# A selective-scan block with a following linear layer: where a chunk's boundary work stands on five engines

## The chip, the cores and the metric

One core of one Trainium2 chip runs the whole program. The metric is the device time of one execution in microseconds (us); a lower one is better. All data are 32-bit floats.

## The reference

For 4096 rows `x` of 1024 values, two blocks follow each other, each with a layer norm ahead of it and the block's input added behind it:

```
x = x + mamba(layernorm(x))          # in_proj -> x, z (2048 channels each)
                                     # xc = silu(causal conv, 4 taps, of x)
                                     # xc @ x_proj -> dt_r (64), B (16), C (16), each rms-normed
                                     # dt = softplus(dt_r @ dt_proj + bias)
                                     # h[t] = exp(dt*A) * h[t-1] + dt*B[t]*xc[t]   (16 states a channel)
                                     # y = (sum_n h*C + D*xc) * silu(z);  out_proj(y)
x = x + layernorm(x) @ W.T + bias    # W dequantised from codes and scales, once
```

## The kernel before

The 4096 rows are cut into 16 **chunks** of 256 rows (`T`), the 2048 channels into 8 **pairs** of 128-channel tiles. The loop runs over 16 x 8 = 128 **steps**; step `S = 8c + j` scans pair `j` of chunk `c`. `first` is j = 0, `last` is j = 7. Four chunks are in work at once: while chunk c is scanned, the step's PE work also holds the input projection and convolution of chunk c+1, the output projection of chunk c-1 and the second linear layer ("ffn") of chunk c-2. Each engine has its own stream of instructions, written out by hand in the order in which it runs; semaphores alone tie them together.

A step has 16 **units** of 512 columns. For each, ACT keeps the last state and makes two exponentials (`unit(u)`, L1107 and L1111), POOL makes the products of dt, x and B (`dbx`, L494, one for two units), DVE scans (`scan(u)`, L1416, into one of four banks `hb`) and multiplies by C (`product(u)`, L1364); `unit(u)` waits for `product(u-4)`, which frees its bank. POOL adds pairs of products (`half`, L512 and L518), and PE sums them over the identity into `ys` (`group(k)`, three for either tile, L606). The last three groups of a step stand in the next one (`late_groups`). The sum times silu(z) is the output (`y_gate`, L1375): tile 0 at the end of its own step, tile 1 early in the next (`late_y`).

PE's other work of a step, by line: `ffn` L721 (DVE adds its result, `add_ffn`, L1332), `out_proj` L799 in parts of the contraction into `g1` (`add_out`, also L1332), `x_proj` L636 (DVE: `pair_ss`, L1310 and L1313), `x_in_proj` L626 in two halves (ACT: `x_taps`, L984 to L992; DVE: `taps`, six operations on L1298), `dt_proj` L656 (ACT: `dt_softplus`, with a table load ahead and behind), and `z_in_proj` L646, the step's last, which may overwrite its bank once `y_gate(S, 0)` has read it. ACT's `silus` takes z's result early in the next step.

At a chunk's **boundary** more is done. In the last step: four transposes of a normed row block (`norm1`, L613, copied by ACT on L976), the statistics of the second norm on DVE (L1339, L1272), and the rms norm of dt, B and C (`rms_apply`, `ss_transpose`, `ss_out`), after which SP writes B and C out and loads them back over all partitions, a quarter at a time (`load_b`, `load_c`, 512 KB each). In the first step: the second norm's start (L946 to L952), its two rows into `xrow` (L959) and four transposes (`norm2`). All transposes go through bank `gx`, one after the other: each waits for ACT's copy of the one before. `edge` marks a last step with `norm1` and a first step with `norm2`. There are 13 boundaries that have both (the last steps of chunks 1 to 13).

SP issues its loads in program order and stops at each wait: what stands behind a waiting load waits as well.

Of the kernel before, what the change touches and what calls it, by code (L numbers as in the profile page):

```python
# [91 lines left out]
def build_program(nc, x, win, wout, wf_codes, wf_scales, ffn_bias, xproj, dtw_in, convw_in, convb_in,  # L92
                  alog_in, dparam_in, lnw_in, out):
    ctx = ExitStack()
    with ctx:
# [179 lines left out]
        def _(sp):  # L275
# [75 lines left out]
            def iteration(st, c):  # L351
# [4 lines left out]
                def step(j):  # L356
# [24 lines left out]
                    if first and st.norm1:  # L381
# [3 lines left out]
                        sp.dma_start(xrow[:], x_rows[c + 2]).then_inc(xrow_in, 16)  # L385
                    if last and st.inproj:
                        bc_rows(c + 1)
                        for q in range(2):
                            load_b(c + 1, q)
                            load_c(c + 1, q)  # L390
                    if nx.x_job(nx_last):
                        load_pair(S + PAIRS + 2)
# [206 lines left out]
        def _(pe):  # L599
# [95 lines left out]
            def iteration(st, c):  # L695
                def step(j):
# [86 lines left out]

                    def out_proj(part):
                        if not st.outproj:
                            return
                        if part == 0:
# [7 lines left out]
                        for kt in range(part * TILES // 4, (part + 1) * TILES // 4):  # L795
# [8 lines left out]
                        if part == 3:  # L804
                            mm.then_inc(o_mm, 1)
# [16 lines left out]
                    if last and st.norm1:  # L822
                        norm1(0)
                        x_proj()
                        out_proj(0)
                        norm1(1)
                        out_proj(1)
                        norm1(2)
                        out_proj(2)
                        norm1(3)  # L830
                        x_in_proj(0)
                        ss_transpose()
                        out_proj(3)
                        dt_proj()
                        x_in_proj(1)
                        group(0)
                        group(1)
                        group(2)
                    elif first and st.ffn:
                        out_proj(0)  # L840
                        out_proj(1)
                        x_proj()
                        out_proj(2)
                        norm2(0)
                        out_proj(3)
                        norm2(1)
                        group(0)
                        dt_proj()
                        norm2(2)
                        group(1)  # L850
                        norm2(3)
                        x_in_proj(0)
                        group(2)
                        x_in_proj(1)
                    else:
                        out_proj(0)
                        out_proj(1)
# [7 lines left out]
                        out_proj(2)  # L865
                        group(2)
                        out_proj(3)
                    z_in_proj(1)
# [70 lines left out]
        def _(act):  # L939
# [144 lines left out]
            def iteration(st, c):  # L1084
                def step(j):
# [88 lines left out]
                    def norm2_row(tt):  # L1174
                        if first and st.ffn:

                            act.wait_ge(l1_tr, after(4 * min(c + 2, NC)))
                            norm2_rows(c - 2, tt)

# [21 lines left out]
                    unit(0)  # L1201
                    unit(1)
                    unit(2)
                    norm2_start()
                    unit(3)
# [4 lines left out]
                    first_skip_term()  # L1210
                    norm1(0)
                    unit(5)
                    norm1(1)
                    rms_square()
                    unit(6)
                    norm2_row(0)
                    norm1(2)
                    unit(7)
                    norm2_row(1)
                    norm1(3)  # L1220
                    unit(8)
                    norm2(0)
                    rms_apply()
                    norm1_start()
                    unit(9)
                    norm2(1)
                    norm1_row(0)
                    unit(10)
                    ss_out()
                    norm2(2)  # L1230
                    norm1_row(1)
                    unit(11)
                    norm2(3)
                    unit(12)
                    if not edge:
                        x_taps()
# [4 lines left out]
                    unit(14)  # L1241
                    if edge:
                        x_taps()
                    unit(15)

                steps(c, step)
# [3 lines left out]
            LAST = NC * PAIRS  # L1250
            norm2_begin(NC - 2)
            act.wait_ge(l1_tr, after(4 * NC))
            act.wait_ge(l2_tr, after(4 * (NC - 2)))
            for tt in range(TT):
                norm2_rows(NC - 2, tt)
            act.wait_ge(f_mm, after(LAST - 2 * PAIRS))
# [11 lines left out]
        def _(dve):  # L1268
# [128 lines left out]
            def iteration(st, c):  # L1397
                def step(j):
# [112 lines left out]
                    product(11)  # L1511
                    y_gate(S, 0)
                    if not edge:
                        taps()
# [6 lines left out]
                    if edge:  # L1521
                        taps()
                    scan(15)
# [84 lines left out]
```

## Time and profile before

| | |
|---|---|
| median of 3 runs | 4553.35 us (4550.11 to 4554.59) |
| profiled execution: time / span | 4553.78 us / 4552.0 us |
| a plain step (2, 3, 4, 6) of chunks 2 to 13, median | 32.26 us |
| last step, median | 37.16 us |
| first step, median | 35.98 us |
| second step, median | 33.58 us |
| PE busy / DVE busy, share of the span | 94% / 91% |
| first scan / last scan's end | 130.3 us / 4411.7 us |

A step's length is the distance between the starts of its first scan and of the next step's. The times in the rows are microseconds from the span's start. A row by stretch has the stretch and its length, the busy us (and count) of PE, PE's weight loads, DVE, ACT and POOL, the mean granted clock, the DMA engines' busy share and GB/s. A row of a timeline has start, duration, engine, line and instruction, count, and the idle time before it with what ended it; PE's counts are passes, two for each matmul, and neighbours overlap by 0.1 to 0.2 us. PE = TensorE matmul, DVE = VectorE, ACT = ScalarE, POOL = GpSimd, SP = SyncE.

### The profile page before, as it was taken

What the parts mean: (1) busy time and instruction counts of PE and PEld (TensorE: products, weight loads), DVE (VectorE), ACT (ScalarE), POOL (GpSimd) and SP (SyncE); (2) the same over time, 40 slices, a digit from 0 to 9 for tenths busy, and PEclk for the clock granted to TensorE, in tenths of its full rate; (3) what the DMA queues carried; (4) which work ended last, traced back from release to release, by engine and by line L of the source; (5) the groups of instructions that cost most, each with busy time, mean ns of one, the idle gap of its engine ahead of it and who ended that gap; (6) DMA issues with size and microseconds to landing.
All of it is one profiled execution on the core that took longest, in us unless ns stands there. A gap on an engine that the chain in (4) does not pass through costs nothing.

```text
span 4552.0 us, 77871 instructions
## 1 busy us (share of the span) xinstructions
PE 4257.0 (94%) x25632; PEld 3830.9 (84%) x25632; DVE 4156.6 (91%) x5745; ACT 3534.8 (78%) x8848; POOL 3887.0 (85%) x2894
## 2 busy tenths in 40 slices
PE   7688989999999999999999999999999999998879
PEld 6567778888888888888888888988888898897769
DVE  3899999999999999999999999999999999999871
ACT  3788787888888788787888888787888878888750
POOL 0898989989898998989899898998989899899870
PEclk9788999999999999999999999999999999998889
DMA  7545556575756657575575757557575665755452
GB/s 247 160 122 184 150 183 184 164 224 174 220 166 196 192 174 220 163 227 163 176 218 165 234 155 219 175 156 242 155 226 168 209 189 147 226 167 178 133 150 85
DMA packets 201348, 828.91 MB, mean 182 GB/s; under 512 B 25456, under 2 KB 34416, under 8 KB 151792
## 3 DMA queue, kind: packets, MB, share of 16 engines
q1 hardware_dynamic: 141296, 639.35, 38.6%
q0 software_dynamic: 41216, 151.01, 18.7%
q10 hardware_dynamic: 18432, 33.56, 2.0%
q8 instruction: 204, 3.34, 0.3%
q14 instruction: 200, 1.64, 0.1%
HBM read 634.57 MB, written 55.05 MB: 151 GB/s over the span
## 4 chain that ended last, share of the span: by engine, by line
PE 60%; POOL 19%; DVE 10%; issue 7%; ACT 2%; DMA 1%; SPq 0%; POOLq 0%; DVEq 0%; ACTq 0%
PE ys L646 14%; POOL dbx L494 12%; PE gx L626 12%; PE ys L606 12%; PE g L799 10%; PE g L721 7%; DVE hb L1416 6%; POOL half L518 3%; POOL half L512 3%; DVE gx L1298 1%; PE ys L636 1%; PE hb L901 1%; DVE hc L1364 1%; DMA ybuf<-in_wf_scales 1%; POOL hd L507 1%
## 5 line engine op out<-in xcount | busy, mean ns | idle before, releaser
L494 POOL TENSOR_TENSOR dbx<-dtx,bb 128x1024 f32<-128x1024 f32 x1024 | 2427.4, 2370 | 231.1 <-DVE hb L1416 183.8
L1416 DVE TENSOR_TENSOR_SCAN hb<-hb,dbx 128x512 f32<-128x512 f32 x2048 | 2495.6, 1219 | 55.4 <-ACT hb L1111 27.3
L1111 ACT ACTIVATE hb<-dt,a_neg 128x256 f32<-128x256 f32 x4096 | 1789.1, 468 | 66.3
L606 PE MATMUL ys<-half,ident 128*128 128x256 f32 x3072 | 811.6, 400 | 162.6 <-POOL half L512 93.6
L799 PEld LDWEIGHTS g<-wo,ybuf 128*128 128x128 f32 x7680 | 919.2, 194 | 30.7 <-issue 14.7
L646 PE MATMUL ys<-xnT,wz 128*128 128x256 f32 x4096 | 926.2, 385 | 11.4 <-DVE ybuf L1375 11.4
L799 PE MATMUL g<-wo,ybuf 128*128 128x128 f32 x7680 | 928.3, 277 | 8.4 <-issue 8.4
L626 PE MATMUL gx<-xnT,wx 128*128 128x256 f32 x3968 | 895.4, 383 | 21.5 <-issue 10.9
L646 PEld LDWEIGHTS ys<-xnT,wz 128*128 128x128 f32 x4096 | 782.6, 193 | 127.8 <-DVE ybuf L1375 22.8
L626 PEld LDWEIGHTS gx<-xnT,wx 128*128 128x128 f32 x3968 | 750.6, 192 | 127.3 <-issue 14.3
L606 PEld LDWEIGHTS ys<-half,ident 128*128 128x128 f32 x3072 | 567.4, 195 | 302.2 <-POOL half L512 125.0
L1107 ACT COPY hstate<-hb 128x2 f32<-128x2 f32 x2044 | 319.0, 156 | 646.1 <-DVE hc L1364 549.3
L518 POOL TENSOR_TENSOR half<-hc 128x512 f32<-128x512 f32 x512 | 651.3, 1272 | 97.0 <-DVE hc L1364 96.8
L1364 DVE TENSOR_TENSOR hd<-hb,cb 128x512 f32<-128x512 f32 x1024 | 688.4, 672 | 0.0
L1364 DVE TENSOR_TENSOR hc<-hb,cb 128x512 f32<-128x512 f32 x1024 | 688.0, 672 | 0.0
L721 PEld LDWEIGHTS g<-wf,x2nT 128*128 128x128 f32 x3552 | 414.1, 192 | 5.7
L721 PE MATMUL g<-wf,x2nT 128*128 128x128 f32 x3552 | 414.5, 275 | 0.0
L512 POOL TENSOR_TENSOR half<-hd 128x512 f32<-128x512 f32 x256 | 326.0, 1273 | 2.5 <-DMA hd<-hd 2.4
L1298 DVE SCALAR_TENSOR_TENSOR gx<-xpre,convw,gx 128x256 f32<-128x256 f32 x744 | 302.2, 481 | 23.2 <-ACT gx L992 23.2
L507 POOL DMA_DIRECT2D hd<-hd x256 | 227.9, 890 | 21.4 <-DVE hd L1364 7.6
L537 POOL TENSOR_TENSOR dtx<-dt,xcs 128x510 f32<-128x510 f32 x128 | 202.4, 1581 | 0.0
L1375 DVE TENSOR_TENSOR ybuf<-ys,gate 128x256 f32<-128x256 f32 x256 | 107.4, 419 | 99.7 <-PE ys L606 95.0
(108 smaller groups left out, 3145.5 us busy)
## 6 DMA issues: line engine op xcount, KB each, us to landing
wz<-in_win SPq DMA_DIRECT2D x128, 1024.0 KB, 5.0
hd<-hd POOLq DMA_DIRECT2D x256, 512.0 KB, 6.3
wx<-in_win SPq DMA_DIRECT2D x124, 1024.0 KB, 5.0
wo<-in_wout SPq DMA_DIRECT2D x123, 1024.0 KB, 7.3
wf<-wf_scratch SPq DMA_DIRECT2D x113, 512.0 KB, 3.6
xc_scratch<-xcn ACTq DMA_DIRECT2D x128, 256.0 KB, 2.7
xcs<-xc_scratch SPq DMA_DIRECT2D x128, 256.0 KB, 5.2
bb<-bc_scratch SPq DMA_DIRECT2D x64, 512.0 KB, 9.6
```

What stands on the lines that cost most here:

```text
L494: nc.gpsimd.tensor_tensor(dbx[:, k % 2, :].rearrange("p (n t) -> p n t", n=NQ), dtx[:, S % 2, a, :].unsqueeze(1).to_broadcast([P, NQ, T]), ...
L512: nc.gpsimd.tensor_tensor(sum_place(SUMS * S + PAIR_SUM[a]), hd[:, 2 * a, 0:HALF], hd[:, 2 * a, HALF:GW], ALU.add).then_inc(halves, 1)
L518: nc.gpsimd.tensor_tensor(sum_place(SUMS * S + LATER_SUMS[a][i]), hc[:, i, 0:HALF], hc[:, i, HALF:GW], ALU.add).then_inc(halves, 1)
L606: mm = nc.tensor.matmul(ys[i // 3][:, 0:T], ident[:], half[:, n % PLACES, w * T:(w + 1) * T], start=False, stop=(i % 3 == 2 and w == 1), s ...
L626: mm = nc.tensor.matmul(pair_bank(q)[:, a * T:(a + 1) * T], pair_weights(q)[:, kk, a * P:(a + 1) * P], xnT[:, chunk % 2, kk, :], start=(kk ...
L646: mm = nc.tensor.matmul(ys[0][:, a * T:(a + 1) * T], wz[:, kk, a * P:(a + 1) * P], xnT[:, q // PAIRS % 2, kk, :], start=(kk == 0), stop=(k ...
L721: mm = nc.tensor.matmul(g1[:, tt * P:(tt + 1) * P], x2nT[:, kk, tt * P:(tt + 1) * P], wf[:, kk, :], start=(kk == 0), stop=(kk == KH - 1))
L799: mm = nc.tensor.matmul(g1[:, tt * P:(tt + 1) * P], ybuf[:, (1 - st.parity) * PAIRS + kt // 2, (kt % 2) * T + tt * P:(kt % 2) * T + (tt + ...
L1111: ins = nc.scalar.activation(h[:, m * T:(m + 1) * T], dt[:, j % 2, a, :], ACT.Exp, scale=a_neg[:, ds((2 * j + a) * N + 2 * v + m, 1)])
L1298: nc.vector.scalar_tensor_tensor(bank[:, a * T:(a + 1) * T], xpre[:, a, tap:tap + T], convw[:, ds((2 * jq + a) * KC + tap, 1)], bank[:, a ...
L1364: nc.vector.tensor_tensor(dst[:, w * UW:(w + 1) * UW], hb[u % 4][:], cb[:, n:n + 2, :].rearrange("p n t -> p (n t)"), ALU.mult).then_inc(h ...
L1416: nc.vector.tensor_tensor_scan(h[:], h[:], dbx[:, k % 2, w * UW:(w + 1) * UW], 0.0, ALU.mult, ALU.add).then_inc(scans, 1)
```

## The change

Four streams are reordered; no arithmetic is added or removed.

- **PE, last step:** the third part of the output projection is split around the last transpose; the second half of the input projection follows the first directly; the fourth part goes from ahead of `dt_proj` to behind the groups, just ahead of z.
- **PE, first step:** the transposes of the second norm start the step's own part, one ahead of each part of the output projection; `x_proj` moves behind the third transpose; the fourth part goes to the end, ahead of z.
- **ACT:** the second norm's start and first row move from the first step to the end of the last one; its second row moves to behind `unit(1)`; its copies move from units 8 to 11 to units 4 to 7. In the last step `x_taps` moves from behind `unit(14)` to behind `unit(12)`.
- **DVE, edge steps:** `y_gate(S, 0)` moves from behind `product(11)` to behind `product(12)`, and `add_out` with the statistics from behind `product(12)` to behind `product(13)`. In the last step the taps move from behind `product(13)` to behind `product(11)`.
- **SP, last step:** the order is B0 B1 C0 B2 C1 B3, wo, dtw, C2, wx, C3, wz; before it was B0 C0 B1 C1, wx, wo, dtw, B2 C2 B3 C3, wz.

```diff
                     if last and st.inproj:
                         bc_rows(c + 1)
-                        for q in range(2):
-                            load_b(c + 1, q)
-                            load_c(c + 1, q)
-                    if nx.x_job(nx_last):
+                        load_b(c + 1, 0)
+                        load_b(c + 1, 1)
+                        load_c(c + 1, 0)
+                        load_b(c + 1, 2)
+                        load_c(c + 1, 1)
+                        load_b(c + 1, 3)
+                    if not last and nx.x_job(nx_last):
                         load_pair(S + PAIRS + 2)
...
                     if last and st.inproj:
-                        for q in range(2, NQ):
-                            load_b(c + 1, q)
-                            load_c(c + 1, q)
+                        load_c(c + 1, 2)
+                    if last and nx.x_job(nx_last):
+                        load_pair(S + PAIRS + 2)
+                    if last and st.inproj:
+                        load_c(c + 1, 3)
...
-                    def norm2_start():
+                    def norm2_first_row():
+                        if last and st.outproj:
+                            norm2_begin(c - 1)
+                            act.wait_ge(l1_tr, after(4 * min(c + 3, NC)))
+                            norm2_rows(c - 1, 0)
+                    def norm2_second_row():
                         if first and st.ffn:
-                            norm2_begin(c - 2)
+                            norm2_rows(c - 2, 1)
...
                     scan(12)
                     product(11)
-                    y_gate(S, 0)
                     if not edge:
+                        y_gate(S, 0)
+                    if not edge or last:
                         taps()
                     scan(13)
                     product(12)
-                    add_out()
-                    norm_stats()
+                    if edge:
+                        y_gate(S, 0)
+                    else:
+                        add_out()
+                        norm_stats()
                     scan(14)
                     product(13)
                     if edge:
+                        add_out()
+                        norm_stats()
+                    if edge and not last:
                         taps()
```

PE's rows of one last step and the following first step (`g<-wo` is the output projection, `gx<-ident,xrow` the transposes, `gx<-xnT,wx` and `ys<-xnT,wz` the two input projections, `ys<-half` the groups). Before:

```order
274 L799 MATMUL g<-wo,ybuf 128x128 x8
275 L613 MATMUL gx<-ident,xrow 128x128 x4
276 L626 MATMUL gx<-xnT,wx 128x256 x8
277 L663 MATMUL ys<-ident,ssn 97x128 x2
278 L799 MATMUL g<-wo,ybuf 128x128 x8
279 L656 MATMUL ys<-ssmT,dtw 128x256 x2
280 L626 MATMUL gx<-xnT,wx 128x256 x8
281 L606 MATMUL ys<-half,ident 128x256 x6
282 L646 MATMUL ys<-xnT,wz 128x256 x16
```

The same place in the changed kernel:

```order
275 L806 MATMUL g<-wo,ybuf 128x128 x4
276 L619 MATMUL gx<-ident,xrow 128x128 x4
277 L806 MATMUL g<-wo,ybuf 128x128 x4
278 L632 MATMUL gx<-xnT,wx 128x256 x8
279 L669 MATMUL ys<-ident,ssn 97x128 x2
280 L632 MATMUL gx<-xnT,wx 128x256 x8
281 L662 MATMUL ys<-ssmT,dtw 128x256 x2
282 L612 MATMUL ys<-half,ident 128x256 x6
283 L806 MATMUL g<-wo,ybuf 128x128 x8
284 L652 MATMUL ys<-xnT,wz 128x256 x16
```

The groups (L606, now L612) no longer stand directly ahead of z; a part of the output projection is between them. DVE's rows of the same last step, from scan 12's product on (`hb<-hb,dbx` is a scan, `ybuf` the gate, `gx<-xpre` the taps). Before:

```order
628 L1364 TENSOR_TENSOR hd<-hb,cb 128x512
629 L1375 TENSOR_TENSOR ybuf<-ys,gate 128x256
630 L1416 SCALAR_TENSOR_TENSOR hb<-hb,dbx 128x512
631 L1364 TENSOR_TENSOR hc<-hb,cb 128x512
632 L1332 TENSOR_TENSOR x<-g,x 128x2x128
633 L1339 BN_STATS bst<-x 128x6 x2
634 L1272 BN_AGGR mv<-bst 128x2 x2
635 L1416 SCALAR_TENSOR_TENSOR hb<-hb,dbx 128x512
636 L1364 TENSOR_TENSOR hc<-hb,cb 128x512
637 L1298 SCALAR_TENSOR_TENSOR gx<-xpre,convw,gx 128x256 x6
```

In the changed kernel:

```order
628 L1369 TENSOR_TENSOR hd<-hb,cb 128x512
629 L1303 SCALAR_TENSOR_TENSOR gx<-xpre,convw,gx 128x256 x6
630 L1421 SCALAR_TENSOR_TENSOR hb<-hb,dbx 128x512
631 L1369 TENSOR_TENSOR hc<-hb,cb 128x512
632 L1380 TENSOR_TENSOR ybuf<-ys,gate 128x256
633 L1421 SCALAR_TENSOR_TENSOR hb<-hb,dbx 128x512
634 L1369 TENSOR_TENSOR hc<-hb,cb 128x512
635 L1337 TENSOR_TENSOR x<-g,x 128x2x128
636 L1344 BN_STATS bst<-x 128x6 x2
637 L1277 BN_AGGR mv<-bst 128x2 x2
```

The gate now stands behind the six taps, a scan and a product. On ACT, at the end of a last step (`xrow<-x` is the second norm's row, the copies of L1107 and L1115 start a unit), the changed kernel has:

```order
883 L1119 ACTIVATE hb<-dt,a_neg 128x256 x2
884 L954 ACTIVATE nmr<-mv 128x2
885 L955 ACTIVATE rstd<-mv,eps_ln 128x2
886 L957 ACTIVATE rstd<-rstd 128x2
887 L960 ACTIVATE nmr<-nmr,rstd 128x1 x2
888 L967 ACTIVATE xrow<-x,nmr,rstd 128x1024
889 L1115 COPY hstate<-hb 128x2
890 L1119 ACTIVATE hb<-dt,a_neg 128x256 x2
```

Rows 884 to 888 stood in the first step before; now they are ahead of that step's first exponentials (row 890).

## Rows read from the trace of the kernel before

**Rows 1.** The page: the chain that ended last, by engine.
```profile
PE 60%; POOL 19%; DVE 10%; issue 7%; ACT 2%; DMA 1%; SPq 0%; POOLq 0%; DVEq 0%; ACTq 0%
```

**Rows 2.** By stretch: a plain step, chunk 7's last, chunk 8's first and second.
```profile
2342.00:2374.30 32.30, 31.89 (x199) 29.13 (x198) 32.14 (x45) 25.96 (x65) 30.15 (x23) 1.00 0.56 165
2236.00:2273.30 37.30, 35.98 (x232) 32.55 (x231) 33.77 (x51) 30.32 (x80) 30.64 (x24) 1.00 0.56 176
2273.30:2308.50 35.20, 31.59 (x191) 27.71 (x190) 31.95 (x44) 30.93 (x76) 31.73 (x26) 1.00 0.99 331
2308.50:2342.10 33.60, 33.19 (x207) 30.51 (x207) 32.21 (x46) 26.10 (x65) 30.08 (x23) 1.00 0.61 187
```

**Rows 3.** Timeline of PE, that boundary: start, us, instruction, count, idle before and releaser.
```profile
2250.88 3.69 PE L626 MATMUL gx<-xnT,wx 128*128 128x256 f32 x16 [0.72 <-issue]
2254.63 1.95 PE L799 MATMUL g<-wo,ybuf 128*128 128x128 f32 x16
2260.74 2.75 PE L606 MATMUL ys<-half,ident 128*128 128x256 f32 x12
2264.01 7.17 PE L646 MATMUL ys<-xnT,wz 128*128 128x256 f32 x32 [0.52 <-DVE ybuf L1375]
2271.02 3.73 PE L721 MATMUL g<-wf,x2nT 128*128 128x128 f32 x32
...
2302.28 7.07 PE L646 MATMUL ys<-xnT,wz 128*128 128x256 f32 x32
```

**Rows 4.** Timeline of DVE, the same boundary.
```profile
2236.13 1.22 DVE L1416 TENSOR_TENSOR_SCAN hb<-hb,dbx 128x512 f32<-128x512 f32 x1
2254.80 1.23 DVE L1416 TENSOR_TENSOR_SCAN hb<-hb,dbx 128x512 f32<-128x512 f32 x1 [1.13 <-ACT hb L1111]
2256.53 1.22 DVE L1416 TENSOR_TENSOR_SCAN hb<-hb,dbx 128x512 f32<-128x512 f32 x1
2263.53 0.42 DVE L1375 TENSOR_TENSOR ybuf<-ys,gate 128x256 f32<-128x256 f32 x1 [1.77 <-PE ys L606]
2269.23 2.43 DVE L1298 SCALAR_TENSOR_TENSOR gx<-xpre,convw,gx 128x256 f32<-128x256 f32 x6
2273.30 1.22 DVE L1416 TENSOR_TENSOR_SCAN hb<-hb,dbx 128x512 f32<-128x512 f32 x1
```

**Rows 5.** Timeline of ACT, the same boundary.
```profile
2258.12 1.28 ACT L1038 ACT_TABLE_LOAD   x1
2261.39 0.16 ACT L1107 COPY hstate<-hb 128x2 f32<-128x2 f32 x1
2264.18 0.18 ACT L984 COPY xpre<-xhist 128x6 f32<-128x6 f32 x1
2266.00 0.17 ACT L1107 COPY hstate<-hb 128x2 f32<-128x2 f32 x1
2274.42 0.19 ACT L946 ACTIVATE nmr<-mv 128x2 f32<-128x2 f32 x1
2275.57 0.16 ACT L1107 COPY hstate<-hb 128x2 f32<-128x2 f32 x1
2276.66 1.28 ACT L1117 ACT_TABLE_LOAD   x1
2283.74 1.23 ACT L959 ACTIVATE xrow<-x,nmr,rstd 128x1024 f32<-128x1024 f32 x1
```

**Rows 6.** PE in chunk 0's last step, chunk 1's last, and a stretch of that.
```profile
369.54 6.54 PE L626 MATMUL gx<-xnT,wx 128*128 128x256 f32 x16 [0.81 <-issue]
627.03 3.30 PE L606 MATMUL ys<-half,ident 128*128 128x256 f32 x8 [2.35 <-POOL half L512]
628.00:631.40 3.40, 3.40 (x12) 2.62 (x12) 1.99 (x4) 3.34 (x7) 2.50 (x2) 0.51 0.27 100
```

**Rows 7.** Waits of POOL for B: the third quarter at boundaries 7 and 9.
```profile
2278.47 0.21 POOL L472 TENSOR_TENSOR bb<-carried,inflow 128x4 f32<-128x4 f32 x1 [0.71 <-DMA bb<-bc_scratch]
2815.57 0.21 POOL L472 TENSOR_TENSOR bb<-carried,inflow 128x4 f32<-128x4 f32 x1 [2.00 <-DMA bb<-bc_scratch]
```

More of the change, by code:

```diff
@@ L782, in z_in_proj, with out_proj @@
                         pair_z(S + 1, a)
-                    def out_proj(part):
+                    def out_proj(lo, hi):
                         if not st.outproj:
                             return
-                        if part == 0:
+                        if lo == 0:
                             pe.wait_ge(wo_in, landed(PAIRS // 2 + S - PAIRS + 1))
@@ L794, in out_proj @@
                                 g1_after_o()
-                        for kt in range(part * TILES // 4, (part + 1) * TILES // 4):
+                        for kt in range(lo, hi):
                             for tt in range(TT):
@@ L803, in out_proj @@
                                                       stop=(kt == TILES - 1), skip_group_check=True)
-                        if part == 3:
+                        if hi == TILES:
                             mm.then_inc(o_mm, 1)
@@ L824, in step @@
                         x_proj()
-                        out_proj(0)
+                        out_proj(0, 4)
                         norm1(1)
-                        out_proj(1)
+                        out_proj(4, 8)
                         norm1(2)
-                        out_proj(2)
+                        out_proj(8, 10)
                         norm1(3)
+                        out_proj(10, 12)
                         x_in_proj(0)
                         ss_transpose()
-                        out_proj(3)
+                        x_in_proj(1)
                         dt_proj()
-                        x_in_proj(1)
                         group(0)
@@ L838, in step @@
                         group(2)
+                        out_proj(12, 16)
                     elif first and st.ffn:
-                        out_proj(0)
-                        out_proj(1)
+                        norm2(0)
+                        out_proj(0, 4)
+                        norm2(1)
+                        out_proj(4, 8)
+                        norm2(2)
                         x_proj()
[L843 to L846, printed above, removed]
+                        norm2(3)
+                        out_proj(8, 12)
+                        x_in_proj(0)
                         group(0)
                         dt_proj()
-                        norm2(2)
+                        x_in_proj(1)
                         group(1)
-                        norm2(3)
-                        x_in_proj(0)
                         group(2)
-                        x_in_proj(1)
+                        out_proj(12, 16)
                     else:
-                        out_proj(0)
-                        out_proj(1)
+                        out_proj(0, 4)
+                        out_proj(4, 8)
                         x_proj()
@@ L864, in step @@
                         group(1)
-                        out_proj(2)
+                        out_proj(8, 12)
                         group(2)
-                        out_proj(3)
+                        out_proj(12, 16)
                     z_in_proj(1)
@@ L1168, in norm1 @@
                             norm_evac(xnT[:, st.parity], 4 * (c + 2), i, gx, l1_tr, l1_evac)
-                    def norm2_start():
-                        if first and st.ffn:
-                            norm2_begin(c - 2)
[L1174 to L1178, printed above, removed]
+                    def norm2_first_row():
[4 more added lines that the diff above has]
+                    def norm2_second_row():
+                        if first and st.ffn:
+                            norm2_rows(c - 2, 1)
                     def norm1_start():
@@ L1202, in step @@
                     unit(1)
+                    norm2_second_row()
                     unit(2)
-                    norm2_start()
                     unit(3)
@@ L1211, in step @@
                     norm1(0)
+                    norm2(0)
                     unit(5)
                     norm1(1)
+                    norm2(1)
                     rms_square()
                     unit(6)
-                    norm2_row(0)
                     norm1(2)
+                    norm2(2)
                     unit(7)
-                    norm2_row(1)
                     norm1(3)
+                    norm2(3)
                     unit(8)
-                    norm2(0)
                     rms_apply()
@@ L1229, in step @@
                     ss_out()
-                    norm2(2)
                     norm1_row(1)
                     unit(11)
-                    norm2(3)
                     unit(12)
-                    if not edge:
+                    if not edge or last:
                         x_taps()
@@ L1241, in step @@
                     unit(14)
-                    if edge:
+                    if edge and not last:
                         x_taps()
                     unit(15)
+                    norm2_first_row()
                 steps(c, step)
@@ L1250, in _ @@
             LAST = NC * PAIRS
[L1251 to L1255, printed above, removed]
+            norm2_rows(NC - 2, 1)
             act.wait_ge(f_mm, after(LAST - 2 * PAIRS))
@@ L1511, in step @@
                     product(11)
-                    y_gate(S, 0)
                     if not edge:
+                        y_gate(S, 0)
+                    if not edge or last:
                         taps()
@@ L1521, in step @@
                     if edge:
+                        add_out()
+                        norm_stats()
+                    if edge and not last:
                         taps()
```

1 line of the change is left out of this document (removed).

## The prediction

> **What bounds the kernel now.** The page's chain comes first: 60% of the time that ended last is PE, 19% POOL, 10% DVE [rows 1]. That is an average. The stretches say more [rows 2]. In a plain step PE is busy 31.9 of 32.3 us and DVE 32.1: both are full, and nothing that only moves work can help there. In the last step PE is busy 36.0 of 37.3 and DVE 33.8; in the first, 31.6 and 32.0 of 35.2; in the second, 33.2 and 32.2 of 33.6. So over these three steps PE has about 100.8 us of work in 106.1, DVE 97.9. At most 5.3 us a boundary can be had (13 boundaries, 69 us, 1.5%), PE is the scarcer of the two, and a wait taken from DVE and given to PE is a loss.
>
> The timelines of one boundary (chunk 7 to 8) show where the 5.3 us go. On PE [rows 3]: 0.72 ahead of the first half of `x_in_proj`, which waits for ACT's copy of the last transpose, and 0.52 ahead of z, which waits for the gate; the rest lies in the first step (POOL's sums, the normed row, copies) up to z at 2302.28. On DVE [rows 4]: 1.13 at scan 9 behind ACT's `rms_apply`, 1.77 at the gate, which waits for group 2, PE's last before z.
>
> **The change, part by part.** I replay the boundary with the durations of its own rows. A unit on DVE (scan and product) is 1.72 (2254.80 to 2256.53) [rows 4].
>
> *Last step, PE up to the groups.* The last transpose stands half a part earlier. A part of `out_proj` starts at 2254.63 and lasts 1.8 net of the overlap with its successor [rows 3], so it is 0.9 earlier; its copy on ACT is then bound by the unit ahead of it and comes 0.7 earlier, and the other half part covers the wait of 0.72. `x_in_proj` starts at 2250.15 for 2250.88. Its halves (3.5 each, 3.69 with the overlap [rows 3]) and the small transpose run on to 2257.5. `dt_proj` (0.9) and the groups (2.6 net [rows 3]) end at 2261.0, for 2263.5. The part behind them ends at 2262.8.
>
> *Last step, ACT and DVE.* ACT's unit 8 and `rms_apply` come 0.7 earlier. DVE's scan 9 starts at 2254.07 for 2254.80. Four units later, at 2260.95, DVE is at the taps. ACT's `x_taps` waits for `x_in_proj`, 2257.5, and takes 1.8 (2264.18 to 2266.00 [rows 5]); the table load, softplus and load that now follow take 3.3 (2258.12 to 2261.39 [rows 5]), unit 13 another 1.1: its exponentials are there at 2263.8. DVE's taps take 2.35 (six operations, 2.43 with the overlap [rows 4]), to 2263.3; it waits 0.5, does scan 13 and product 12, and the gate ends at 2266.0. Before, it ended at 2263.95.
>
> *So z starts at 2266.05 for 2264.01, and PE waits 3.2 us ahead of it* where it waited 0.52. This is the price of the later gate: 2.35 of taps and 1.7 of unit are now ahead of a result for which PE stands still.
>
> *The clock.* PE lost its clock in chunk 1 after shorter waits: a wait of 2.35 was followed by a stretch at a granted clock of 0.51, that is 1.2 for 2.4 GHz, in which two groups and the next lines up to 631.4 were stretched; the two groups alone took 3.30 [rows 6] for 1.9 (three take 2.75 [rows 3]). I take 1.5 us for the fall, from that difference of 1.4 and a little work behind it. The bounds are nothing (no fall, and the sum is 0.25 better at each boundary, no more, since ACT is late there too) and 3.0: in chunk 0's last step, behind several waits between small matmuls, half of an `x_in_proj` took 6.54 [rows 6] for 3.69 [rows 3]. The Trainium skill, page "TensorE: Matmul & The Clock Gate", Part 1, says that half rate is the array's default and that only activity releases the gate. The rows agree, and by either a new wait of PE costs more than its length.
>
> *The second norm's first row.* DVE's statistics end at 2269.7, and its step at 2271.3 (two units and the gate's shifts). ACT waits for the statistics, then needs 1.15 for the norm's start (2274.42 to 2275.57 [rows 5]), 1.15 for a row (1.23 with the overlap [rows 5]) and 1.05 for unit 0: first scan at 2273.1. DVE waits 1.8 us there, which it never did, and the last step comes out at 37.0, as long as before (2236.13 to 2273.30 [rows 4]): what the earlier taps give, the row takes. Behind it ACT runs without a break: unit 1, second row, units 2 and 3 to 2277.15, the two table loads and the silus 3.7 (2276.66 on [rows 5]) to 2280.9, unit 4 and the skip term to 2282.3, and the copy of the first transpose to 2282.9.
>
> *First step, PE.* From 2266.05: z 7.0 (to 2271.02 from 2264.01), ffn 3.55, late groups 2.7 [rows 3], the fall 1.5: 2280.8. First transpose to 2281.25; the first part must wait for DVE's late gate, 2281.35; it ends at 2283.2, and the copy is there. Transpose, part, transpose, `x_proj` end at 2286.9. DVE stands at `pair_ss` from 2286.4: a wait of 0.5 that is new, since `x_proj` is later by half a step's front. From scan 6 at 2287.25 DVE has seven units to 2299.3, waits 0.4 for ACT's unit 13 (softplus as before), scan and product, and the gate ends at 2301.85. PE, with no normed row to wait for (1.2 before) and all copies in time, has its last part done at 2301.5. z starts at 2301.9 for 2302.28 [rows 3]: 0.4 gained, 0.1 of it lost again to restarting PE behind a wait. The second step is then PE's, as before (33.2 of 33.6 busy [rows 2]), and passes the gain on.
>
> *B's rows.* At this boundary POOL waited 0.71 for B's third quarter; at boundary 9, 2.00 [rows 7]. I counted all 13, these two being rows of them: 0.71 is the least, 1.5 the mean. The third quarter now has 1.5 MB ahead of it instead of 2 MB of rows and 2 MB of weights, is issued by 2258 and is needed at 2276: the wait goes at every boundary. My replay of boundary 7 has it covered already; the others gain the further 0.8 on average, because their first step is that much longer (median 35.98, here 35.2). What moves behind: wo has 3 MB ahead of it as before; wx and C2 are issued some 6 us later and needed 15 us after that. I cost them at nothing; if wx were late, the first half of `x_in_proj` would wait, us for us.
>
> **Sum.** 0.3 + 0.8 = 1.1 us at each of 13 boundaries: 14 us. Against it stand two edges outside them: chunk 0's last step has no output projection to fill PE, so the later gate delays z by nearly 4 us there, and in chunk 15's first step likewise; I take 1.5 us for each, less than the delay, since DVE bounds what follows. 4553.8 - 14 + 3 = 4542.8 us for the profiled execution; it stands 0.4 above the median, so 4543 (rounded up, as a replay leaves out small latencies).
>
> **Rivals.** A difference of 9 us, 0.2%, is about what measurement can tell from none.
> 1. *PE's wait decides: slower.* The fall lasts longer, or z starts later still. Another 1.5 to 1.7 us on z, ffn or groups passes on whole from 2280.8 on, since PE leads the chain there: late gate, scan 3, `x_proj`, scan 6. Per boundary 1.1 - 1.7 = -0.6; 13 x 0.6 + 3 = 11: 4564 us. The gain is gone once the fall costs 2.4 us for my 1.5. For it: chunk 0's 6.54 [rows 6]. Against: a single wait amid dense work, as here, had the short one.
> 2. *Only B's rows count.* The replay's 0.3 is nothing or -0.4; then 0.8 x 13 - 3 less up to 5: 4545 to 4551, no difference.
> 3. *No fall, and the edges cost nothing.* 1.35 x 13 = 17.5: 4536.
> 4. *PE is filled.* If DVE's order fitted PE's, the 5.3 us would go: 4553 - 13 x 4 = 4501. Against it stands the gate behind taps and unit.
> 5. *B's rows don't come earlier,* because POOL's accumulating transfers share the engines with them. Then 0.3 x 13 - 3 = 1: 4553, no change. Against it: 2.00 us of wait [rows 7] behind 4 MB of SP's own, of which 2.5 MB are now behind B. The Trainium skill, "DMA: Bandwidth & Descriptors", Issuing engines are not separate DMA queues, says that DMAs issued by all engines run on the same 16 DMA engines and interleave; no run here shows yet how far that goes.
>
> **Chances.** Forecast (4538 to 4547) 0.38; rival 1 0.24; rivals 2 and 5 0.20; rival 3 0.13; rival 4 0.05. Faster by over 0.2%: four fifths of the forecast's 0.38 (its upper end is above 4544), rivals 3 and 4: 0.50 rounded. Slower: 0.23. Same, the rest: 0.27. The range reaches from between rivals 3 and 4 to near rival 1: 4528 to 4562.
>
> **What would show it.** In the changed trace: a wait of PE ahead of z in the last step of 3 us, with a granted clock near 0.5 behind it (right), or under 1.5 (the gate is earlier than I say); last step 37.0, first 34.5, second 33.9; DVE's first scan of the first step behind ACT by 1.8; no wait of POOL for B's third quarter; scan 9's wait 1.0; DVE at `pair_ss` 0.5. I am wrong if the clock's fall lasts longer, if ACT gets the statistics much earlier than 2269.7, or if a load moved back (wx, C3) is awaited.

## The result, and the profile after

The change made the kernel slower: 4605.39 us (median of 5, 4598.50 to 4613.16) against 4553.35 (median of 5, 4550.11 to 4557.14); ratio 1.0113, interval 1.0102 to 1.0124. The forecast was 4543, and the time lies outside its range. The profiled execution took 4600.62 us (span 4598.8), 46.8 of span more than before.

The page's chain of the changed kernel, by engine, for [rows 1], and one of its groups:

```profile
PE 57%; POOL 23%; issue 8%; DVE 7%; ACT 3%; DMA 1%; SPq 0%; POOLq 0%; DVEq 0%; ACTq 0%
...
L518 POOL TENSOR_TENSOR half<-hd 128x512 f32<-128x512 f32 x256 | 325.7, 1272 | 66.2 <-DMA hd<-hd 66.2
```

POOL has grown by 4 points. Its sum of a pair (`pair_sum`, L518) now waits 66.2 us in all for the accumulating DMA hd<-hd. Before, the sum of a pair hardly waited for it (0.1 us on average at a boundary, 5.0 now). The same boundary as in [rows 2], chunk 7's last step and chunk 8's first and second:

```profile
2258.94:2295.98 37.04, 33.68 (x202) 30.15 (x202) 33.62 (x51) 31.64 (x84) 32.37 (x24) 0.95 0.57 184
2295.98:2330.91 34.93, 34.26 (x217) 31.35 (x216) 31.80 (x43) 29.69 (x72) 29.58 (x26) 1.00 0.92 316
2330.91:2369.54 38.63, 35.50 (x209) 31.82 (x208) 32.20 (x45) 26.10 (x65) 30.36 (x23) 0.96 0.59 172
```

The last two steps of the three were forecast as 34.5 and 33.9. The first step is 0.4 off; the second is 5 us longer than before, with a granted clock of 0.96. Timeline of PE there, for [rows 3]:

```profile
2288.85 8.86 PE L652 MATMUL ys<-xnT,wz 128*128 128x256 f32 x32 [3.28 <-DVE ybuf L1380]
...
2317.26 3.62 PE L632 MATMUL gx<-xnT,wx 128*128 128x256 f32 x16
...
2324.93 7.17 PE L652 MATMUL ys<-xnT,wz 128*128 128x256 f32 x32 [0.54 <-DVE ybuf L1380]
2331.95 3.73 PE L727 MATMUL g<-wf,x2nT 128*128 128x128 f32 x32
2335.52 1.03 PE L612 MATMUL ys<-half,ident 128*128 128x256 f32 x4
2339.68 3.30 PE L612 MATMUL ys<-half,ident 128*128 128x256 f32 x8 [3.13 <-POOL half L518]
```

The wait of 3.28 ahead of z is the forecast one. That of 3.13 in the second step is not: two groups of `half` stand still behind POOL and then take 3.30. Two stretches of PE behind the two waits (columns as in [rows 2]; the clock is the third number from the end):

```profile
2289.30:2292.70 3.40, 3.40 (x10) 2.69 (x9) 3.33 (x8) 0.29 (x3) 2.50 (x3) 0.51 1.04 284
2339.60:2343.00 3.40, 3.33 (x10) 2.42 (x11) 0.00 (x0) 0.39 (x1) 3.40 (x3) 0.62 0.48 184
```

Both times PE, having stood still, went on slowly: at a granted clock of 0.51 in the first of these stretches, 1.2 for 2.4 GHz, and of 0.62 on average in the second. What POOL waited for, by the timelines of POOL and of the DMAs that SP issues:

```profile
2320.47 1.21 POOL L531 DMA_DIRECT2D x<-in_ffn_bias  x1
...
2323.56 1.37 POOL L513 DMA_DIRECT2D hd<-hd  x1
...
2338.36 1.26 POOL L518 TENSOR_TENSOR half<-hd 128x512 f32<-128x512 f32 x1 [5.14 <-DMA hd<-hd]
```

```profile
2320.91 0.33 SPq L280 DMA_DIRECT2D wx<-in_win  x1
2324.42 0.33 SPq L399 DMA_DIRECT2D wo<-in_wout  x1
```

And the same place before:

```profile
2295.53 1.17 POOL L525 DMA_DIRECT2D x<-in_ffn_bias  x1
...
2298.62 1.34 POOL L507 DMA_DIRECT2D hd<-hd  x1
```

```profile
2302.48 0.33 SPq L280 DMA_DIRECT2D wx<-in_win  x1
2302.86 1.19 SPq L395 DMA_DIRECT2D wo<-in_wout  x1
```

Before, POOL had issued both of its transfers (the bias of 1024 KB, hd of 512 KB) before SP loaded wx (1024 KB), 3.9 us behind the second. Now wx goes out 0.4 us behind the bias and ahead of hd: the second half of `x_in_proj`, which frees its buffer, ends at 2320.9. From issue to landing the accumulation hd<-hd takes, before and after:

```profile
DMA to landing us min/median/max: 8.7/8.7/8.7
```

```profile
DMA to landing us min/median/max: 14.7/14.7/14.7
```

and the bias 8.0 and 13.6. hd lands at 2323.6 + 14.7 = 2338.3, where `pair_sum` starts. What the DMA engines moved in between is seen by queue: packets, MB, share of the 16 engines' time (a packet counts whole in the stretch in which it starts, so this can pass 100%). `q1` holds SP's loads, `q0 software_dynamic` POOL's transfers. Before, from 2299 to 2304, while the bias moves:

```profile
q0 software_dynamic: 276, 1.07, 107.4%
```

After, from 2321.2 to 2325.3, just behind the bias and wx, and from 2328 to 2332, when wo is under way too:

```profile
q1 hardware_dynamic: 116, 0.94, 76.3%
```

```profile
q0 software_dynamic: 104, 0.43, 53.1%
q1 hardware_dynamic: 100, 0.82, 50.6%
```

In the first of the two only SP's queue moves, and that is wx: its first packet comes 1.0 us behind its issue, the first of the bias 5.2 us behind its own (4.9 to 5.2 at the 13 boundaries, by the packets of the trace; 1.9 to 3.4 before). In the second the bias shares the engines with wo. hd, next in POOL's queue, lands 4.2 us behind the bias. The list of waits of the changed kernel (total, times, longest):

```profile
PE ys L652 <- DVE ybuf L1380: 58.4, 34, 5.1
...
POOL half L518 <- DMA hd<-hd: 66.2, 15, 5.6
```

Over the 13 boundaries, last steps are shorter by 2.9 us in sum, first steps by 13.7, second steps longer by 61.0 (4.7 each); the rest of the span is longer by 2.4. Together 46.8. The forecast passed over a column of [rows 2]: in chunk 8's first step the DMA engines were busy for 0.99 of the time, in its neighbours for 0.56 and 0.61.

### The profile page after: what moved, and what is told of

The parts are those of the page before. It is cut to its first block, busy times and chain, and to the rows that moved or that the text cites. A ratio compares the mean times of both kernels' runs of the same rounds, so it can differ in the third digit from the quotient of the medians.

```text
span 4598.8 us, 77871 instructions
## 1 busy us (share of the span) xinstructions
PE 4279.0 (93%) x25632; PEld 3859.2 (84%) x25632; DVE 4154.7 (90%) x5745; ACT 3535.2 (77%) x8848; POOL 3886.5 (85%) x2894
## 4 chain that ended last, share of the span: by engine, by line
PE 57%; POOL 23%; issue 8%; DVE 7%; ACT 3%; DMA 1%; SPq 0%; POOLq 0%; DVEq 0%; ACTq 0%
PE ys L652 15%; POOL dbx L500 14%; PE ys L612 11%; PE g L806 10%; PE gx L632 9%; PE g L727 7%; DVE hb L1421 4%; POOL half L524 4%; POOL half L518 3%; PE ys L642 1%; POOL hd L513 1%; PE hb L909 1%; DVE hc L1369 1%; DVE gx L1303 1%; DMA ybuf<-in_wf_scales 1%
## 5 line engine op out<-in xcount | busy, mean ns | idle before, releaser
L652 PE MATMUL ys<-xnT,wz 128*128 128x256 f32 x4096 | 947.5, 391 | 58.4 <-DVE ybuf L1380 58.4
L612 PE MATMUL ys<-half,ident 128*128 128x256 f32 x3072 | 816.7, 403 | 172.4 <-POOL half L518 111.4
L806 PEld LDWEIGHTS g<-wo,ybuf 128*128 128x128 f32 x7680 | 932.2, 195 | 23.7 <-issue 5.0
L652 PEld LDWEIGHTS ys<-xnT,wz 128*128 128x128 f32 x4096 | 795.5, 197 | 179.2 <-DVE ybuf L1380 68.8
L806 PE MATMUL g<-wo,ybuf 128*128 128x128 f32 x7680 | 939.6, 278 | 2.1 <-issue 0.6
L1115 ACT COPY hstate<-hb 128x2 f32<-128x2 f32 x2044 | 318.6, 156 | 683.2 <-DVE hc L1369 516.5
L612 PEld LDWEIGHTS ys<-half,ident 128*128 128x128 f32 x3072 | 576.4, 198 | 310.1 <-POOL half L518 142.0
L518 POOL TENSOR_TENSOR half<-hd 128x512 f32<-128x512 f32 x256 | 325.7, 1272 | 66.2 <-DMA hd<-hd 66.2
```

What stands on the lines that cost most here:

```text
L518: nc.gpsimd.tensor_tensor(sum_place(SUMS * S + PAIR_SUM[a]), hd[:, 2 * a, 0:HALF], hd[:, 2 * a, HALF:GW], ALU.add).then_inc(halves, 1)
L612: mm = nc.tensor.matmul(ys[i // 3][:, 0:T], ident[:], half[:, n % PLACES, w * T:(w + 1) * T], start=False, stop=(i % 3 == 2 and w == 1), s ...
L652: mm = nc.tensor.matmul(ys[0][:, a * T:(a + 1) * T], wz[:, kk, a * P:(a + 1) * P], xnT[:, q // PAIRS % 2, kk, :], start=(kk == 0), stop=(k ...
L806: mm = nc.tensor.matmul(g1[:, tt * P:(tt + 1) * P], ybuf[:, (1 - st.parity) * PAIRS + kt // 2, (kt % 2) * T + tt * P:(kt % 2) * T + (tt + ...
```

## The experiments

Two theories. **A:** the load of wx slows POOL's transfers, hd lands late, POOL and PE wait in the second step; z's wait costs little. **B:** z's wait and the clock behind it, both in the last step, are the loss. The first expectation names a third, **C:** hd lands late because POOL issues it later. Each run was timed beside the kernel before (its medians there: 4552.53 for e1 to e4, 4553.51 for e5 to e8, 4549.94 for e9 and e10).

**e1, wx issued later by one product.** In the changed kernel, ahead of `load_pair` (wx):

```diff
+                        if first and st.ffn:
+                            sp.wait_ge(hcs, after(UNITS * S + 12))
                         load_pair(S + PAIRS + 2)
```

> The changed kernel, but in each first step SP waits for DVE's product 11 before it issues the load of wx (and so wo behind it), some 4 us later than the changed kernel does. Theory A (collision): wx and wo, issued right behind POOL's bias transfer, slow that transfer and the accumulation behind it, for which pair_sum of the second step waits 5 us. Then the accumulation's flight falls from 14.7 us to 10 to 12, the second step from 38.8 to 35 to 37, and the time to 4555 to 4580. Theory B (the gate): PE's wait of 3.3 us ahead of z and the clock's fall behind it cost the 50 us; then nothing changes here, 4600. Theory C: the accumulation is late because POOL issues it 2 us later; nothing changes here either.

Measured: 4570.73 (ratio 1.0042, 1.0027 to 1.0057). wx goes out 1.4 us later on average, not 4, and wo no later; hd's flight falls from 14.5 to 13.0 (means), the second step's median from 38.8 to 36.0. That small shift turns the order round: wx now goes out 2.0 us behind the bias (0.4 before this edit), and the bias has its first packet 1.9 us behind its issue, ahead of wx's. The bias's flight falls from 14.2 to 10.7, and wx's rises from 5.8 to 11.4.

**e2, wx issued behind the gate.** The same place, another wait:

```diff
+                        if first and st.ffn:
+                            sp.wait_ge(y_ready, after(2 * S + 1))
                         load_pair(S + PAIRS + 2)
```

> The changed kernel, but in each first step SP waits for the gate of tile 0 before it issues the load of wx, some 6.5 us later than the changed kernel. Theory A: the accumulation's flight falls to about 9 us as in the kernel before, PE's wait in the second step (2.2 to 3.6 us) is gone or under 0.5, the second step is 34 to 35, and the time 4540 to 4556; a smaller part of it can come back as a wait of PE for wo. Theories B and C: 4600, as PE's wait ahead of z in the last step (3.3 us) is untouched.

Measured: 4547.19 (0.9988, 0.9979 to 0.9998). wx goes out 4.4 us later than in the changed kernel, and wo, which stands behind it, 1.2 us. POOL's wait for hd, in the list of waits, is down to a quarter, and the second step (the stretch below) to 33.93 in the median:

```profile
POOL half L520 <- DMA hd<-hd: 16.4, 15, 2.4
```

```profile
2301.23:2335.56 34.33, 33.84 (x209) 30.67 (x208) 32.20 (x46) 26.09 (x65) 30.39 (x23) 1.00 0.65 207
```

One wait in SP's queue gives 58 us back (4605.39 - 4547.19), with the later gate untouched. POOL issues the bias and hd as late in the first step as in the changed kernel (24.8 us into it on average, 24.5 there, for the bias), so C is out.

**e3, the gate of last steps back behind product 11.** In the changed kernel:

```diff
                     scan(12)
                     product(11)
-                    if not edge:
+                    if not edge or last:
                         y_gate(S, 0)
-                    if not edge or last:
                         taps()
                     scan(13)
                     product(12)
-                    if edge:
+                    if edge and not last:
                         y_gate(S, 0)
-                    else:
+                    if not edge:
                         add_out()
                         norm_stats()
```

> The changed kernel, but in the last steps the gate of tile 0 stands behind product 11 again, ahead of the taps; first steps keep the later gate. PE's wait of 3.3 us ahead of z and the clock's fall behind it should go. Theory B: 4540 to 4560. Theory A: z comes 3 us earlier, but the first step is held by ACT's row and its copies, so it gains 0.3 to 0.5 us at most, and the collision in the second step stays: 4595 to 4603.

Measured: 4595.68 (1.0097, 1.0081 to 1.0112). z's wait is gone, and little is won: PE's timeline shows it wait in the first step instead, for ACT, and go on slowly (a part of `out_proj` takes 3.33; it is 1.95 elsewhere):

```profile
2299.89 0.66 PE L619 MATMUL gx<-ident,xrow 128*128 128x128 f32 x4 [2.11 <-ACT xcn L1009]
2300.38 3.33 PE L806 MATMUL g<-wo,ybuf 128*128 128x128 f32 x16
```

B is out as the main cause.

**e4, the kernel before with only SP's new order in last steps.** Its diff is the SP part of the change.

> The kernel before, with only SP's new order in the last steps (B's rows ahead of the weights). By my prediction POOL's wait for B's third quarter (1.5 us on average) is gone, the first step falls from 35.98 to about 35.2 and the time to 4543 to 4546. Rival: the wait was covered on the whole, or another load is now late, and the time stays at 4553.

Measured: 4540.98 (0.9977, 0.9967 to 0.9986). The waits of POOL for B's rows, before and here:

```profile
POOL bb L472 <- DMA bb<-bc_scratch: 27.5, 24, 2.4
```

```profile
POOL bb L477 <- DMA bb<-bc_scratch: 4.5, 8, 2.0
```

SP's order alone is worth 4552.53 - 4540.98 = 11.6 us. The median of the first step falls by 0.8, from 35.98 to 35.21, as forecast. In the profiled execution, though, which is 13.1 us shorter, the steps of the 13 boundaries give only 7.8 of it, 0.6 a boundary (chunk 2's first step is 2.1 longer), and 4.0 lie ahead of the first scan and behind the last one, where this edit changes nothing.

**e5, e2 and e3 together.**

> Two edits to the changed kernel at once: in first steps SP waits for the gate of tile 0 before it loads wx, and in last steps that gate stands behind product 11 again, ahead of the taps. If the collision and PE's wait ahead of z were two separate costs, this gives the first's 58 us and the second's 10 us: 4537. If, as I hold, PE then only waits later, for ACT's silus in the first step (2.1 us, seen with the gate alone), the second edit is worth 0 to 5 us here: 4542 to 4548.

Measured: 4541.89 (0.9974, 0.9965 to 0.9984). That is 5.3 us less than e2, at the lower edge of what the second theory said, and the intervals of the two overlap. It cannot be told from e4: all that moved on PE, ACT and DVE is worth nothing yet.

**e6, e5 with the second norm behind ACT's units.** The norm's start and first row leave the front of the first step, where DVE waited 1.82 us for ACT:

```diff
                     unit(0)
                     unit(1)
-                    norm2_second_row()
+                    norm2_first_row()
                     unit(2)
                     unit(3)
+                    norm2_second_row()
...
                     unit(15)
-                    norm2_first_row()
```

> The kernel of the two edits, and on ACT the second norm's start and first row move from the end of the last step to behind unit 1 of the first step, the second row to behind unit 3. Theory: the first step is led by ACT's chain from the statistics over row, units 0 to 3 and silus to the first transpose; units 0 and 1 now run while ACT would wait for the statistics, so the silus come some 2 us earlier, DVE's first scan doesn't wait (1.8 us), the last step is 35.0 to 35.5, and 13 boundaries gain 1 to 2 us each: 4518 to 4534. Rival: PE or POOL's sums take over at once, and it stays within 5 us of the kernel of the two edits.

Measured: 4551.35 (0.9992, 0.9982 to 1.0002). Missed. The last step is 34.93, as expected, but hd is late again: at the boundary from chunk 3 to 4 POOL's timeline has

```profile
1214.74 1.35 POOL L515 DMA_DIRECT2D hd<-hd  x1
...
1231.29 1.26 POOL L520 TENSOR_TENSOR half<-hd 128x512 f32<-128x512 f32 x1 [6.91 <-DMA hd<-hd]
```

although wx goes out 1.3 us behind hd (at 1216.07), the same distance as in e2. So the order of hd and wx alone does not decide; over the boundaries the second step runs from 33.3 to 41.3 with the same order. SP's timeline there shows other loads just ahead of the bias (which goes out at 1211.65):

```profile
1206.96 0.38 SPq L371 DMA_DIRECT2D x<-in_x  x1
1207.44 0.41 SPq L376 DMA_DIRECT2D xcs<-xc_scratch  x1
1207.95 0.38 SPq L380 DMA_DIRECT2D wf<-wf_scratch  x1
1208.41 0.60 SPq L385 DMA_DIRECT2D xrow<-in_x  x1
```

The load of x goes out 4.7 us ahead of the bias here, 10.5 us ahead in e2 (chunk 8's first step), and in the 4 us behind the bias's issue the engines moved nothing but SP's queue:

```profile
q1 hardware_dynamic: 446, 1.57, 104.5%
```

At seven boundaries wf's load is in flight for 2 us or more behind the bias's issue; there the bias's first packet comes 3.8 to 5.4 us behind its issue, its flight is 12.7 to 15.4, and the second step over 39. At the other six the first packet comes after 1.9 to 2.5 us, the flight is 7.6 to 9.2, and the second step at most 34.8. It is theory A with another load in wx's place. Why x goes out late in this kernel was not followed.

**e7, the changed kernel with only the bias transfer earlier** (POOL):

```diff
                     group_sum(S, 0, 0)
+                    if first and st.ffn:
+                        add_bias(c - 2)
                     products(5)
                     group_sum(S, 0, 1)
                     products(6)
                     pair_sum(S, 0)
-                    if first and st.ffn:
-                        add_bias(c - 2)
```

> The changed kernel, with nothing but POOL's bias transfer moved, from behind pair_sum of tile 0 to behind the first group_sum, some 7 us earlier in the first step. wx and wo stay as early as in the changed kernel. If the accumulation is late because it stands behind the bias in POOL's own queue, which wx slows, its flight falls from 14.5 to 7 to 10 us and the time to 4545 to 4560. If wx and wo slow it themselves, its flight stays above 12 and the time above 4580.

Measured: 4547.94 (0.9986, 0.9976 to 0.9995). wx still goes out ahead of hd (boundary 7: 2289.63 against 2292.29), the bias still flies 13.9 us (issued earlier, it meets the loads of x and xrow), and hd, whose flight is 10.2, comes in time. So it is also enough to keep the bias transfer and hd apart in POOL's queue: one moved line, 57 us.

**e8, e6 and e7 together.**

> The kernel with the rows moved (three edits), and the bias transfer moved ahead as well. The accumulation should no longer be awaited at all in the second step; if such waits are still left in the kernel of three edits (0 to 1.2 us a boundary), this takes them: 4515 to 4530. Rival: the earlier bias now collides with the first accumulation or the loads of x and xcs in the middle of the first step, and the time is 5 to 15 us above the kernel of three edits.

Measured: 4510.68 (0.9908, 0.9894 to 0.9923), the fastest of all, and 4 us below what was expected. The three steps of the boundary:

```profile
2214.88:2249.80 34.92, 34.84 (x224) 31.83 (x224) 33.73 (x50) 31.72 (x86) 30.51 (x24) 1.00 0.53 168
2249.80:2284.28 34.48, 32.13 (x196) 28.10 (x195) 31.88 (x44) 29.67 (x71) 30.85 (x25) 1.00 0.98 325
2284.28:2318.31 34.03, 33.85 (x209) 30.65 (x208) 32.20 (x46) 26.09 (x65) 30.95 (x24) 1.00 0.68 218
```

PE is busy 34.84 of 34.92 us in the last step, at full clock.

**e9, the changed kernel with only wo's load behind the gate.** The wait of e2, ahead of wo instead of wx.

> The changed kernel, but in first steps only the load of wo waits for the gate of tile 0; wx is still loaded some 0.4 us behind the bias transfer's issue. The wait changes wo's issue little, since it already comes behind the last part of the output projection. If wx is what slows the bias and with it the accumulation, its flight stays above 13 us and the time at 4590 to 4608. If wo does it, the flight falls to about 11 and the time by over 20 us.

Measured: 4602.6 (1.0113, 1.0096 to 1.0129): no effect. wo moved by only 1 us on average, so this is a weak test of wo; e1, in which wx moved by 1.4 us and wo by none, is the stronger one for wx. The part that wo has in the flights of 14 us stays open.

**e10, e8 with the later gate of the change.**

> The fastest kernel so far (rows moved, bias moved, wx held, 4510.7 us) with one edit undone: in last steps the gate of tile 0 stands behind product 12 again. PE then waits over 3 us ahead of z, with a fall of the clock behind it. In the changed kernel that was hidden by ACT's late chain; here ACT comes 2 us earlier, so by my theory PE leads and the first step grows by 1 to 2.5 us at 13 boundaries: 4522 to 4540. If the wait is hidden here too: 4508 to 4514.

Measured: 4540.72 (0.9982, 0.9972 to 0.9991), 30 us more than e8, and 34 by the ratios, as the two were timed beside different executions of the kernel before. PE's timeline in e10, and the same z in e8:

```profile
2264.72 8.86 PE L654 MATMUL ys<-xnT,wz 128*128 128x256 f32 x32 [3.28 <-DVE ybuf L1385]
```

```profile
2241.32 7.07 PE L654 MATMUL ys<-xnT,wz 128*128 128x256 f32 x32
```

The wait and the slow z cost 2.3 to 2.6 us a boundary once nothing hides them. That is at the upper end of what was expected.

Medians of the steps (first and second ones of chunks 2 to 13), means over the 13 boundaries for the rest:

| | last | first | second | bias's flight | hd's flight | PE's longest wait in the second step | time |
|---|---|---|---|---|---|---|---|
| before | 37.16 | 35.98 | 33.58 | 8.9 | 9.5 | 0.4 | 4553 |
| after | 37.02 | 34.93 | 38.80 | 14.2 | 14.5 | 3.0 | 4605 |
| e1 | 37.03 | 34.54 | 36.00 | 10.7 | 13.0 | 1.4 | 4571 |
| e2 | 37.02 | 34.93 | 33.93 | 7.9 | 10.8 | 0.4 | 4547 |
| e6 | 34.93 | 34.48 | 39.14 | 11.1 | 13.6 | 2.5 | 4551 |
| e7 | 37.02 | 34.92 | 33.93 | 13.5 | 10.3 | 0.4 | 4548 |
| e8 | 34.93 | 34.48 | 33.93 | 10.9 | 10.0 | 0.4 | 4511 |
| e10 | 35.11 | 36.84 | 33.93 | 12.7 | 7.6 | 0.4 | 4541 |

## Why the prediction was wrong

**The step that failed** is "What moves behind": of the DMAs I followed only SP's queue in the last step, and "cost them at nothing". In the first step I let the new order of PE run `x_in_proj` earlier and asked only what PE gains by it ("z starts at 2301.9 for 2302.28"), not what its end releases. It releases wx's buffer, and the load goes out beside POOL's bias transfer. Then "the second step is ... PE's, as before, and passes the gain on" fails: 38.80 us for my 33.9, 61.0 us over the 13 boundaries. My list of what would prove me wrong named a wx that comes too late (the last step's); the first step's came too early. No rival had this; rival 1 ended on the right side, for another reason.

Shown: the delay of wx alone (e1) takes 35 of the 52 us away, the delay of wx with wo 1.2 us later (e2) all of them, and the move of the bias alone (e7) all of them too, in steps that go with PE's wait for the sum behind hd. Of the added 61.0 us in the second steps 54.3 come back in e2. PE's wait there is 3.0 us on average for 0.4 before; at the boundary shown the two groups behind it take 3.30, some 1.4 more than at full clock. The second step is 33.93 for 33.58 in every kernel with the change whose hd comes in time, as I had forecast.

How wx does it, the packets show. In the changed kernel wx's first packet comes 0.4 + 1.0 = 1.4 us behind the bias's issue, and the bias's own would have come after 1.9 (e1, e2). So wx is ahead, and the bias has its first packet only when wx has been moved, at 5.1 us. In e1 it is the other way round: the bias starts first, and wx, for 5.8 us of flight, needs 11.4. The Trainium skill, "DMA: Bandwidth & Descriptors", SWDGE vs HWDGE vs iDMA, says that GpSimd's and SyncE's transfers use different internal queues of the same engines, which take turns. The trace agrees for the stretch from 2328 to 2332, with 104 packets of one queue and 100 of the other, and does not for that from 2321.2 to 2325.3, with 116 of SP's and none of POOL's. Open is what keeps the second transfer's packets back until the first is nearly through; the trace does not show when they were ready.

**The other steps**, by their own numbers:
- z's wait of 3.2: 3.28, at every boundary. The fall of the clock: forecast 1.5, measured 8.86 - 7.17 = 1.7. It followed at 12 of the 13 boundaries: from chunk 10 to 11, behind the same 3.28, z took 7.17 at a granted clock of 1.00. At others it went on longer; by windows of e2 at the end of chunk 8's last step:

```profile
2527.60:2531.00 3.40, 3.40 (x10) 2.68 (x9) 3.33 (x8) 0.41 (x3) 2.25 (x3) 0.50 1.04 295
2531.00:2534.40 3.40, 3.40 (x14) 2.88 (x13) 1.58 (x3) 3.27 (x9) 2.64 (x2) 0.78 1.03 430
```

  The first step behind it took 36.0 for 34.93.
- Last step 37.0: 37.02. DVE's wait of 1.8 for ACT's row: 1.82. `pair_ss` 0.5: 0.54 at most boundaries. Scan 9's wait of 1.0: 0.89.
- First step 34.5: 34.93 in the median.
- Last and first steps together: 14 us forecast, 2.9 + 13.7 = 16.6 measured. Up to the second step the sum held.
- B's rows: forecast 0.8 a boundary; 0.8 by the medians of e4, 0.6 by its sum; POOL's wait for them all but gone.
- The other 0.3 a boundary, from the order on PE, was not found: e2, the whole change with wx held back, is 6.2 us slower than e4, which has SP's order alone.
- The edges: 3 forecast, 2.4 measured outside the boundaries' three steps. The places are others (chunk 0's last step 0.5 shorter, not 1.5 longer; chunk 1's first steps longer), so the number is luck.
- Two sums of mine do not close. The step lengths 37.0, 34.5 and 33.9 are 0.6 us less than boundary 7's 106.0, where I gained 0.3; and rival 4 names 5.3 us and reckons with 4.

With wx out of the way the change gives 4547.19 (e2) against the 4543 of the working. That is nearer than the terms deserve: in e2's trace the three steps of the 13 boundaries give 5.3 us in sum (last -2.9, first -9.1, second +6.7) for my 14; five first steps have the long fall of the clock (6.1 us in sum over 34.93 each). What lies outside them is 0.7 shorter where I charged 3, but 4.6 us were saved ahead of the first scan and behind the last one, where the edit does nothing.

That the later gate was a bad bargain the runs bear out, but how bad depends on what stands beside it: its removal gains 7 to 10 us in e3 and 5 in e5 against e2, both hardly clear of noise, and 30 in e8 against e10.

## What to carry to other kernels

When a part of the work moves earlier, list each buffer that its end frees, the load that waits for that buffer, and what is in flight at the new time; a load that is harmless late can be harmful early. Two transfers that one engine issues behind each other, the second of them awaited, want to be apart: here one moved line was worth 57 us. A wait of PE is to be priced at its length plus the slow stretch behind it, and a gain is judged only once the stall next to it is gone (the same gate was worth 10 us at most in one kernel and 30 in another).

## What was not expected of the hardware

- A 1024 KB load issued 0.4 us behind an accumulating transfer of 1024 KB stretched that transfer from 8.9 to 14.2 us (means over 13 boundaries), and the accumulation of 512 KB behind it from 9.5 to 14.5, while the load itself was faster than before (5.8 for 7.6).
- Issued later, the load overtook: its first packet came 1.0 us behind its issue, where the accumulating transfer took 1.9 at its best, and 5.1 when it was overtaken.
- The effect is steep: 1.4 us of delay for the load took 2.8 us off the second step, and 4.4 us of delay (with wo 1.2 us later) took 4.9 of the 5.2 that had been added.
